# A change of order around each new set of weights in a fused attention kernel: VectorE's third w_lo between two reciprocals, q and k lows ahead of a transposition, TensorE's last weight chunk last

## The reference

```python
xn = _layernorm(x, axis=-1)                      # x: (2, 512, 512)
q = (xn @ Wq.T) ...; k = (xn @ Wk.T) ...; v = (xn @ Wv.T) ...
q = _rmsnorm(q, q_norm_w); k = _rmsnorm(k, k_norm_w)
scores = jnp.einsum('bkgqd,bksd->bkgqs', qg, k) / math.sqrt(HD)
bias = jnp.where(rel > 0, NEG_INF, slopes[:, :, None, None] * rel)
attn = jax.nn.softmax(scores + bias[None], axis=-1)
s = jnp.einsum('bkgqs,bksd->bkgqd', attn, v) ... @ Wo.T
g = _silu(_L0_ffn_ref(xn, A, B, Wr, br))
return x + s * g
```

## Time and profile before

| | |
|---|---|
| median of 3 runs | 741.79 us (741.38 to 743.2) |
| the profiled execution, its own time | 743.02 us |
| its span in the trace | 741.2 us |
| PE busy | 720.8 us (97%) |
| DVE busy | 600.6 us (81%) |
| ACT busy | 559.7 us (76%) |
| POOL busy | 335.6 us (45%) |
| granted TensorE clock, mean | 0.998 of full speed |

### The profile page before, as it was taken

One profiled execution on the slowest core, in us unless ns is written; L12 is line 12 of the kernel. 1 busy time (PEld: TensorE's weight loads), 2 busy tenths in 40 slices (PEclk: granted clock), 3 DMA queues, 4 the chain that ended last, 5 costly groups with the idle time before them and its releaser, 6 DMA issues.

```text
span 741.2 us, 14630 instructions
## 1 busy us (share of the span) xinstructions
PE 720.8 (97%) x3741; PEld 605.4 (82%) x3741; DVE 600.6 (81%) x1490; ACT 559.7 (76%) x1440; POOL 335.6 (45%) x320
## 2 busy tenths in 40 slices
PE   8899999999999999999999999999999999999997
PEld 7787878878788888888888888888888887888776
DVE  6857798678886889787986889777986979878985
ACT  4566888587877877777886978778887768769873
POOL 4223434454434543545444543346326434445556
PEclk9999999999999999999999999999999999999999
DMA  8015968687685778868686786958787785867761
GB/s 304 1 30 140 274 170 235 194 239 224 172 267 160 223 203 229 242 158 254 183 231 198 229 241 173 280 141 232 214 229 217 191 264 147 232 196 204 205 191 72
DMA packets 214773, 148.02 MB, mean 200 GB/s; under 512 B 48992, under 2 KB 205536, under 8 KB 214624
## 3 DMA queue, kind: packets, MB, share of 16 engines
q1 hardware_dynamic: 184224, 130.39, 60.7%
q10 hardware_dynamic: 30528, 17.38, 8.9%
HBM read 85.84 MB, written 61.87 MB: 199 GB/s over the span
## 4 chain that ended last, share of the span: by engine, by line
PE 62%; DMA 10%; DVE 9%; issue 7%; ACT 6%; SPq 2%; POOL 2%; ACTq 1%; DVEq 0%; POOLq 0%
PE out_ps L1363 6%; PE qkv_ps L1363 5%; PE out_ps L1365 5%; PE qkv_ps L1364 5%; PE out_ps L1364 5%; PE qkv_ps L1365 5%; DMA x_sb<-turning 5%; PE score_ps L1363 4%; PE score_ps L1365 3%; PE score_ps L1364 3%; PE mix_ps L1363 3%; PE mix_ps L1365 3%; PE mix_ps L1364 3%; DMA turning<-squared 3%; PE turn_ps L1364 2%
## 5 line engine op out<-in xcount | busy, mean ns | idle before, releaser
L589 POOL TENSOR_TENSOR pt_lo<-x_sb,pt_hi 128x512 fp32r<-128x512 f32 x129 | 164.2, 1296 | 257.5 <-ACT pt_hi L795 257.5
L720 ACT ACTIVATE probs<-probs,neg_max 128x128 f32<-128x128 f32 (+3 forms) x256 | 142.1, 559 | 33.3 <-DVE neg_max L1018 32.1
L1018 DVE CUSTOM_DVE_ANT_0 probs<-score_ps,cst,slope 128x128 f32<-128x128 f32 (+3 forms) x256 | 131.0, 543 | 20.0 <-PE score_ps L1365 19.1
L728 ACT ACTIVATE probs<-probs,recip 128x128 f32<-128x128 f32 (+3 forms) x252 | 126.1, 549 | 8.0 <-DVE recip L1025 8.0
L795 ACT ACTIVATE pt_hi<-x_sb 128x512 fp32r<-128x512 f32 x153 | 86.6, 623 | 50.6 <-issue 31.7
L1363 PE MATMUL qkv_ps<-w_hi,xt_hi 128*128 128x256 f32 (+1 forms) x364 | 118.8, 326 | 2.4 <-DVE xt_lo L961 1.5
L1364 PE MATMUL qkv_ps<-w_lo,xt_hi 128*128 128x256 f32 (+1 forms) x364 | 118.4, 325 | 0.0
L1365 PE MATMUL qkv_ps<-w_hi,xt_lo 128*128 128x256 f32 (+1 forms) x364 | 118.0, 324 | 0.0
L1363 PE MATMUL out_ps<-wo_hi,o_hi 128*128 128x512 f32 x252 | 102.5, 407 | 0.8 <-DVE o_lo L1063 0.6
L1039 DVE STREAM_TRANSPOSE squared<-probs 128x256 f32<-128x256 f32 (+3 forms) x124 | 100.4, 810 | 0.1
L579 POOL TENSOR_TENSOR inv_rms<-sums,minus_half 128x5 f32<-128x5 f32 x64 | 76.9, 1202 | 50.1 <-DVE sums L1077 50.1
(11 more groups left out here) (203 smaller groups left out, 1630.3 us busy)
## 6 DMA issues: line engine op xcount, KB each, us to landing
qk_moved<-turning_qk SPq DMA_DIRECT2D x60, 320.0 KB, 3.4
turning_qk<-qk_squared ACTq DMA_DIRECT2D x212, 80.0 KB, 2.2
turning<-squared SPq DMA_DIRECT2D x120, 128.0 KB, 2.4
x_sb<-turning SPq DMA_DIRECT2D x30, 512.0 KB, 5.2
w_raw<-wqkv SPq DMA_DIRECT2D x32, 384.0 KB, 5.0
turning<-squared SPq DMA_DIRECT2D x120, 96.0 KB, 2.1
x_sb<-turning SPq DMA_DIRECT2D x30, 384.0 KB, 4.2
turning<-squared SPq DMA_DIRECT2D x128, 64.0 KB, 2.0
```

Of the source, the lines that this page charges most:

```text
L589: nc.gpsimd.tensor_tensor(by_quad(pt_lo, j), moved_block(t, j), by_quad(pt_hi, j).bitcast(F32), ALU.subtract).then_inc(pt_lo_by_pool, 1)
L720: nc.scalar.activation(probs[:, h, 0:n], probs[:, h, 0:n], ACT.Exp, bias=neg_max[:, h:h + 1], scale=-1.0, accum_out=total[:, h:h + 1]).the ...
L728: nc.scalar.activation(to[:, h, 0:n], probs[:, h, 0:n], ACT.Copy, scale=recip[:, h:h + 1]).then_inc(probs_ready, 1)
L1018: nc.vector.tensor_tensor_reduce(probs[:, h, 0:n], score_bank(t, h), cst[:, C_DIST + SEQ - n:C_DIST + SEQ], slope[:, h:h + 1], HUGE, ALU.a ...
```

## The change

Four orders are changed; no instruction is added or removed.

```diff
 # POOL, slot(g, t, left)
-                if t % BLOCKS == W_SLOT and here(t + 3, left):
+                if t % BLOCKS == W_SLOT:
                     turned_lo(g, t - 2)
                 if here(t + 2, left):
                     inverse_rms(g, t + 2)
                 if t % BLOCKS == W_SLOT and here(t + 3, left):
                     split_w(g + 1, range(W_DVE, KC))
-                elif t % BLOCKS == W_SLOT:
-
-                    turned_lo(g, t - 2)
 # DVE, w_slot(g, t)
                 reciprocals(g, t, 0)
+                split_w(g + 1, range(W_DVE - 1, W_DVE))
                 reciprocals(g, t, 2)
-                split_w(g + 1, range(W_DVE - 1, W_DVE))
                 normalize_q(g, t + 2)
                 square_both(g, t + 2)
+                turned_qk_lo(g, t + 1)
                 square_probs(g, t, 0)
-                turned_qk_lo(g, t + 1)
                 square_probs(g, t, 2)
 # DVE, slot(g, t, left)
+                if t == 2:
+
+                    turned_qk_lo(g, t + 1)
                 if here(t, left):
                     square_probs(g, t, 0)
-                if here(t + 1, left):
+                if here(t + 1, left) and t > 2:
                     turned_qk_lo(g, t + 1)
 # PE, project_new(g, t)
-                parts = ((q_ps(t), slice(0, QW)), (qkv_ps[:, 1, 0:QKV - QW], slice(QW, QKV)))
-                for k, (to, cols) in enumerate(parts):
-                    if k == 1:
-                        pe.wait_ge(k_norm_ready, ONE(g, t - 1, 1))
-                        pe.wait_ge(v_lo_ready, ONE(g, t - 1, 1))
-                    for c in range(KC):
-                        if k == 0:
+                parts = ((q_ps(t), slice(0, QW), q_ready), (qkv_ps[:, 1, 0:QKV - QW], slice(QW, QKV), kv_ready))
+                first, last = range(0, KC - 1), range(KC - 1, KC)
+                for chunks in (first, last):
+                    for to, cols, _ in parts:
+                        if chunks is first and to is parts[1][0]:
+                            pe.wait_ge(k_norm_ready, ONE(g, t - 1, 1))
+                            pe.wait_ge(v_lo_ready, ONE(g, t - 1, 1))
+                        for c in chunks:
                             pe.wait_ge(w_hi_done, (g + t // BLOCKS) * KC + (c + 1))
-                        pe.matmul(to, xt_hi[:, c, rows], w_hi[:, c, cols], start=c == 0, stop=False)
-                        pe.matmul(to, xt_lo[:, c, rows], w_hi[:, c, cols], start=False, stop=False)
...
```

More of the change, by code:

```diff
@@ new lines, in project_new @@
+                first, last = range(0, KC - 1), range(KC - 1, KC)
[5 more added lines that the diff above has]
+                        for c in chunks:
+                            pe.wait_ge(w_hi_done, (g + t // BLOCKS) * KC + (c + 1))
+                            pe.matmul(to, xt_hi[:, c, rows], w_hi[:, c, cols], start=c == 0, stop=False)
+                            pe.matmul(to, xt_lo[:, c, rows], w_hi[:, c, cols], start=False, stop=False)
+                    for c in chunks:
+                        if c < W_DVE:
+                            pe.wait_ge(w_lo_by_dve, (g + t // BLOCKS - 1) * W_DVE + (c + 1))
+                        else:
+                            pe.wait_ge(w_lo_by_pool, (g + t // BLOCKS - 1) * (KC - W_DVE) + (c - W_DVE + 1))
+                        for to, cols, done in parts:
+                            product = pe.matmul(to, xt_hi[:, c, rows], w_lo[:, c, cols], start=False, stop=c == KC - 1)
+                            if c == KC - 1:
+                                product.then_inc(done, 1)
```

## The result

| | before | after |
|---|---|---|
| median of 8 runs | 741.23 us (739.53 to 743.2) | 745.97 us (743.86 to 748.33) |
| the profiled execution, its own time | 743.02 us | 745.78 us |
| its span in the trace | 741.2 us | 744.0 us |

The ratio is 1.0061, with a 95% interval from 1.0042 to 1.008: 4.5 us more, between 3.1 and 5.9. The prediction was 742.0 us, no difference that a measurement can tell, within 738.6 to 744.6 us; the time lies above that range. It was wrong.

The account below looks back on a forecast made before the run. PE, busy 97% of the span, was taken as the bound, with DVE's queue setting its time at slot 6. 6 x 0.06 + 0.39 - 0.5 + 0 = +0.25 us on 741.79 gave 742.0 us, range 738.6 to 744.6.

Parts of the forecast that it names:

- the measure of the change: In a w slot: the time DVE comes to the second `square_probs` (191.62 before), taken to set PE's time.
- The ordinary w slot, +0.06: Six w slots: `q_lo` starts 0.53 sooner but `square_probs` (0.59) follows it; +0.06 us each, between -0.02 and +0.14.
- The fifth slot's +0.39: Fifth w slot: reciprocals back to back, POOL only 0.10 sooner, `q_lo` 0.20 sooner at best, less 0.59: +0.39 us.
- POOL in the last group, -0.5: Last group: PE no longer held 0.61 us by POOL's `pt_lo`; -0.5 us, between 0 and -0.6.
- Chunk 3 last, 0: PE's projection: the wait for the last `w_hi` (2.9 us) goes, but PE then waits for `k_lo` and DVE's bias; 0.
- Slot 2, 0: Slot 2, once: `q_lo` and `k_lo` of unit 3 ahead of a `square_probs`; 0, between -0.1 and +0.3 us.
- The faster one (POOL does not hold `q_lo`): W slots: `q_lo` starts once `q_hi` is there, DVE 0.39 sooner at the bias; -2.8, 738.9 us; chance 0.20.
- The slower one: W slots: SP's probability writes start 0.9 later and come too late; 745.2 us at a 0.45 shortfall; chance 0.15.
- DVE's cover ahead of the first bias of slot 7: DVE's 0.90 us idle time there, waiting for PE, was taken to absorb SP's writes moving by 0.9; costed at 0.
- x = 0.3: Shortfall of the 0.90 cover in slot 7, lost in each of seven slots; range took it in up to 0.3.
- the bias at 5.3: Profile sign: first bias of slot 6 starts 5.3 us behind the start of ACT's last `w_hi`, as before.
- 0.4 more in the fifth slot: Profile sign: in the fifth w slot the first bias of slot 6 starts 0.4 more behind ACT's last `w_hi`.

## Why the prediction was wrong

**The step that failed** is the measure of the change: "when DVE comes to the second `square_probs` (191.62 before), since everything from there to the bias is unchanged". The list of instructions from there to the bias is unchanged; what POOL does beside them isn't. The prediction asked of `q_lo` and `k_lo` whether POOL stands in their way and didn't ask it of the copy two places behind, which in the kernel before had cleared POOL's `pt_lo` by 0.15 us. It also followed what `square_both` gains (some 0.6 us forecast, 0.77 measured; the 0.88 us that it says DVE waited ahead of the second reciprocal is `w_lo`'s own step, and the row there has 0.62 of idle time) only along DVE, and not through ACT's DMA issues to `pt_hi` and to POOL. The experiments show both: with the copy moved and nothing else, the loss in the w slots is gone, and with POOL unmoved and the copy later it is larger.

**The terms of the sum.** The ordinary w slot, +0.06: up to the `acc` it is +0.09, and the hold of the copy adds 0.42 to 0.47 (0.35 in the first slot), so that the slot is +0.51 to +0.56 (+0.43 in the first): +3.7 for all seven. This mis-sized term is most of the miss; of the rest, slot 2 is the part that the runs support. (The start was off as well: 741.79 is the median of three executions, that of eight is 741.23.) The fifth slot's +0.39: in the profiled execution after, the first reciprocal is early in all seven slots, and the case didn't arise; with the copy moved it arose once, with +0.50. Which slot has it differs from trace to trace. POOL in the last group, -0.5: about -0.6, and -0.1 (-1.3 to +1.2) by the times of that edit alone, so right as far as it can be told. None of DVE's three `pt_lo` blocks is held after, where one took 1.59 before:

```profile
703.91 1.88 DVE L1112 TENSOR_TENSOR pt_lo<-x_sb,pt_hi 128x512 fp32r<-128x512 f32 x3
```

Chunk 3 last, 0: right, 1.0007 with both ends within 0.3%. Slot 2, 0: about +0.8, beyond its own bound of +0.3. The rows of slot 2 after (DVE, then SP):

```profile
67.04 0.84 DVE L1099 STREAM_TRANSPOSE qk_squared<-squares 128x640 f32<-128x640 f32 x1
68.60 0.69 DVE L1048 TENSOR_TENSOR q_lo<-qk_moved,q_hi 128x512 fp32r<-128x512 f32 x1 [0.71 <-ACT q_hi L751]
...
69.47 1.83 DVE L1036 STREAM_TRANSPOSE squared<-probs 128x768 f32<-128x768 f32 x2
70.47 3.90 SPq L485 DMA_DIRECT2D turning<-squared  x8
74.42 0.46 SPq L490 DMA_DIRECT2D qk_moved<-turning_qk  x1
```

The same place before, DVE and SP:

```profile
67.98 0.85 DVE L1102 STREAM_TRANSPOSE qk_squared<-squares 128x640 f32<-128x640 f32 x1
70.02 4.12 SPq L485 DMA_DIRECT2D turning<-squared  x8
74.19 0.45 SPq L490 DMA_DIRECT2D qk_moved<-turning_qk  x1
```

`q_lo` waits 0.71 for ACT, and both transpositions stand behind it. From the start of `square_both`, SP's writes began 2.04 and its read of q and k 6.21 us later; now it is 3.43 and 7.38. The prediction named this cost ("SP's writes of unit 2 start later by about the 0.9") and gave it 0.3 at most; from `square_both` on they start 1.4 later. That these 1.2 us of SP's queue are what the slot loses is argued from the order of the rows; no run moved them alone. That the slot loses at all rests on three comparisons that agree in sign: this edit alone (+1.0, -0.1 to +2.1), and the two pairs of kernels that differ in slot 2 alone (+1.6 with it and +0.3 without, -2.0 with it and -4.7 without).

**The rivals.** The faster one (POOL does not hold `q_lo`) is refuted by 1.13 us for `q_lo` in all seven slots and by the run with `q_lo` in front alone. The slower one is right in its sign and wrong in its mechanism: SP's eight writes did start 0.95 later by A, but ACT's `q_hi` of unit 7 waits only 0.18 us for its DMA (0.22 to 0.41 in the other slots), and DVE's cover ahead of the first bias of slot 7 is whole (0.91, before 0.90). One reason that it is whole is that the held copy has already made that bias late; with the copy moved the late writes eat into the cover, and in one slot of the fourteen in the two kernels with that move they use more than all of it. Its range had a slip: x = 0.3 gives 741.79 + 0.25 + 2.1 = 744.1, not the 744.6 of its upper end. SP, ACT and DVE after, behind the second w slot:

```profile
192.15 3.77 SPq L485 DMA_DIRECT2D turning<-squared  x8
199.31 0.63 ACT L751 ACTIVATE q_hi<-qk_moved 128x512 fp32r<-128x512 f32 x1 [0.18 <-DMA qk_moved<-turning_qk]
203.87 0.75 DVE L1015 CUSTOM_DVE_ANT_0 probs<-score_ps,cst,slope 128x512 f32<-128x512 f32 x1 [0.91 <-PE score_ps L1365]
```

**What was right.** No wait for `w_hi` on PE; POOL's `w_lo` at A + 0.91 (forecast: A + 0.91); `q_lo` at 1.13 (1.1) and its end 0.55 behind POOL's; no wait for POOL in the last group's mix. Two of its tests fail: the bias at 5.3, and 0.4 more in the fifth slot, which is like the others. The wait for `k_lo` did not go either (0.27 in the second slot, 2.8 in all): PE arrives sooner by as much as `k_lo` is there sooner. The Trainium skill's rule (SBUF — State Buffer, "Who interferes with whom") also says that a VectorE copy can contend with GpSimd, when it enters one of the two-port modes. The trace agrees that this copy contends, with 0.15 us clear of POOL and 0.62 beside it; in which mode it ran no run shows. The prediction applied the section to `q_lo` and `k_lo` only.

## What to carry to other kernels

Before calling the rest of a queue unchanged, lay the other engine's instructions over it at their new times: what holds an instruction depends on when the neighbour's instruction runs, and the neighbour moves with the change through every queue it waits for, DMA issues included. Look first for near misses, the pairs that in the trace of before clear each other by a few tenths of a microsecond; a copy of five elements in such a place can cost as much as a large instruction. Small instructions with no deadline belong where the other engine is idle: here that, with the cover for `q_lo` and slot 2 given back, turned 0.6% slower into 0.6% faster.

## What the runs showed of the hardware

In these rows the hold doesn't depend on the size of the held instruction. A copy of 128x5 elements, 0.15 us when alone, took up to 1.22 us because it began just behind a POOL instruction of 1.28 us. Who is first decides: 0.10 us behind cost the copy 1.06, and 0.14 ahead cost nothing on either engine (the copy took 0.15, POOL's `pt_lo` 1.29 as always). The end of the hold was about the same for the copy as for the subtractions, some 0.1 us before POOL's recorded end. For the copy: in the second w slot after, 193.22 + 0.62 - 0.15 = 193.69 against 192.52 + 1.29 = 193.81, and with `q_lo` in front 196.94 + 0.92 - 0.15 = 197.71 against 196.56 + 1.28 = 197.84. For `q_lo` after, with its 0.65 when not held: 190.11 + 1.13 - 0.65 = 190.59 against 188.83 + 1.86 = 190.69. Not held were the transposition (0.67 us under POOL's `w_lo`) and the bias, which reads its scores from `score_ps` (0.62 us beside a `pt_lo` that began 0.07 sooner, 0.60 alone). That stands for these forms of instruction; others weren't tried.
